# Scattering expert outputs with an add onto zero-filled rows in HBM, in place of a plain write

## The chip, the cores and the metric

The kernel runs on 1 core of one Trainium2 chip. The metric is the device time of one execution in microseconds (us), the median of the runs shown. All arithmetic is fp32; matrix products of fp32 operands are made from a high and a low part.

## The reference, cut to what matters

One layer: attention with a residual and a layer norm, then a mixture of experts with a shared expert, a residual and a layer norm. There are 2048 tokens of 512 features and 64 experts; each token goes to 6 of them, and an expert takes at most 256 rows.

```python
scores = jax.nn.sigmoid(x_flat @ w_gate)
_, topk_idx = jax.lax.top_k(scores, TOPK)                 # TOPK = 6
w = ...                                                   # scores of the six, divided by their sum
x_disp = jnp.zeros((E, CAP, C), x.dtype).at[flat_e, pos].set(x_flat[token_ids], mode='drop')
up = jnp.einsum('ecd,edh->ech', x_disp, w_up)
g_r, v_r = jnp.split(up, 2, axis=-1)
out_r = jnp.einsum('ech,ehd->ecd', jax.nn.silu(g_r) * v_r, w_down)
y_ts = jnp.where(valid[:, None], out_r[flat_e, pos_c], 0.0)
routed = (y_ts.reshape(N, TOPK, C) * w[:, :, None]).sum(axis=1)
x = _layernorm(x + shared + routed)
```

## The kernel before

**Attention and routing** (to about 1007 us). Attention runs over 8 chunks of 256 tokens. After each chunk its tokens are normalized, gated and ranked, and GpSimd (POOL) scatters each token's row (512 features and 6 codes, 518 words) into `disp_hbm`, where each expert has 256 row places; these are the 96 dispatch scatters of line 693. `disp_hbm` is zero-filled earlier, and so is `y_hbm`, the table of 12288 rows (one for each token and choice) of 512 words, in 48 transfers from `zero_hbm` (line 616).

**Experts** (about 1007 to 1242 us). The loop runs over items `n`: 6 groups of the shared expert, then the 64 experts. SyncE (SP) issues all loads on one queue (q1), in an order written out by hand (lines 626 to 640): the rows of an expert (`load_rows`, 518 KB, 8 buffers), its up weights (`load_up`, 256 KB, 20 buffers), and the down weights of two experts (`load_down`, 256 KB, 6 buffers). TensorE (PE) turns an expert's rows (`flip`, line 1589), multiplies them by the up weights (line 1391) and, for a pair of experts at a time, by the down weights (line 1637). ScalarE (ACT) and VectorE (DVE) split operands into high and low parts; POOL makes the low part of every second expert's up weights (line 776), DVE that of the others. ACT (line 960) and DVE (line 1329) copy the down product of an expert from its bank into one of four `y_out` buffers; they first wait for the scatters that last read the buffer (`y_free`, line 338).

POOL then scatters `y_out`: two instructions for an expert, 128 in all, each for 128 rows of 512 words (line 787, queue q0). The row number in `y_hbm` comes from the codes that travelled with the token; a place of the expert that holds no token has a number beyond `bounds_check` and is left out. 12288 of the 16384 places hold a token, and each number occurs once. Before its first scatter POOL waits until the zero fill of `y_hbm` is done (line 782). In POOL's own queue the scatters of a pair stand between the subtractions of line 776.

**Shared groups put off, and the end** (1234 us to the end). Two shared groups run after the experts. SP waits for all scatters (line 644), then loads the six rows of each token from `y_hbm`, 16 tiles of 128 tokens with 1536 KB each (line 648, 7 buffers). PE and DVE weight and add them (lines 1677 and 1356), and the last layer norm and the stores follow.

Of the kernel before, what the change touches and what calls it, by code (L numbers as in the profile page):

```python
# [11 lines left out]
ALU = mybir.AluOpType  # L12
# [18 lines left out]
def side_step(jobs):  # L31
    for job in jobs[:]:
        if next(job, "over") == "over":
            jobs.remove(job)


def build(nc, x, x_t, Wq, bq, Wk, bk, Wv, bv, Wo, bo, w_gate, w_sup, w_sdown, w_up, w_down, out):
# [21 lines left out]
    with ctx:  # L59
# [3 lines left out]
        def sem(name):  # L63
            return ctx.enter_context(nc.semaphore(name))
# [175 lines left out]
        d_y = [sem(f"dma_y{b}") for b in range(NY)]  # L240
# [9 lines left out]
        def outputs_at(n):  # L250

            if n >= NI - 1:
                return range(n - 1, n)
            return range(n - 2, n) if n >= SH + 2 and n % 2 == 0 else range(0)
# [52 lines left out]
        def low_by_dve(g):  # L307

            return g >= NU and g % 2 == 1
# [8 lines left out]
        def y_made(e, g, t):  # L318

            if t or g % 2:  # L320
                e.wait_ge(a_y, g + 1)
            else:
                e.wait_ge(v_y, g // 2 + 1)
# [94 lines left out]
        def split_at(n):  # L418

            g = n if n < NU else n + NU - SH if n >= SH else -1  # L420
            return range(g, g + 1) if 0 <= g < E else range(0)
# [231 lines left out]
        def gpsimd(e):  # L653
# [116 lines left out]
            for n in range(-LEAD, NI + 1):  # L770
                for g in split_at(n):
                    if not low_by_dve(g):
                        e.wait_ge(a_uphi, g + 1)
                        if g >= NU:
                            e.wait_ge(p_up, SH + g - NU + 1)
                        e.tensor_tensor(up_lo[g % NU][:, :, :], up_w[g % NW][:, :, :],
                                        up_hi[g % NU][:, :, :].bitcast(F32), ALU.subtract).then_inc(g_wlo, 1)
                side_step(jobs)
                side_step(jobs)
                for i in outputs_at(n):  # L780
                    if i == SH:
                        e.wait_ge(d_yzero, 16 * NZ)
                    g, y = i - SH, i % NY
                    e.wait_ge(v_rowat, 2 * (g // 2) + 2)
                    for t in range(2):
                        y_made(e, g, t)
                        e.indirect_dma_start(  # L787
                            y_hbm, bass.IndirectOffsetOnAxis(row_at[:, 2 * g + t:2 * g + t + 1], 0),
                            y_out[y][:, t, :], None, bounds_check=T * TOPK - 1,
                            oob_is_err=False).then_inc(d_y[y], 16)  # L790
                side_step(jobs)

            for n, part in enumerate(FINAL):
# [887 lines left out]
        block = ctx.enter_context(nc.Block())  # L1681
        block.sync(sync)
        block.gpsimd(gpsimd)
        block.scalar(scalar)
        block.vector(vector)
# [42 lines left out]
```

## Time and profile before

| | us |
|---|---|
| median of 2 runs | 1312.22 (1311.82 to 1312.63) |
| the profiled execution | 1323.67 |
| its span, first to last instruction | 1321.9 |
| PE busy, share of the span | 96% |
| DVE / ACT / POOL busy | 76% / 69% / 41% |
| read from HBM / written to HBM | 177.87 MB / 134.91 MB |

The span is what all views of the trace are counted in; a window is given in us from the span's start. A busy PE is not a PE at its peak. The DMA share is the mean busy share of the 16 DMA engines of the core. The queues are q1 for all that SP issues, q0 for the indirect transfers of POOL, q10 for the stores that ACT issues at the end. The profiled execution is longer than the median of the runs by 11.5 us, so changes of time are worked out within it.

### The profile page before, as it was taken

The page shows a single profiled execution, that of the slowest core. Times are in us where ns is not written, and L with a number is a line of the kernel's source. Part 1 is how long each engine was busy: PE and PEld are TensorE (multiplying, and loading weights), DVE is VectorE, ACT ScalarE, POOL GpSimd, SP SyncE. Part 2 cuts the span into 40 slices and gives each one's busy share as a digit, 9 for nine tenths or more (in the row PEclk, how much of TensorE's full clock was granted, in tenths as well). Part 3 has the DMA queues.
Part 4 walks back from the last instruction along what each step waited for, and adds up shares of the span by engine and source line. Part 5 has one row for each costly group of instructions (what it writes and reads, how often), then busy time and mean ns, then how long its engine had stood idle before and what let it go on. Part 6 is the DMA issues. An engine that isn't in the chain of part 4 may idle for free. (4 is left out here: it accounts for less than half of the span.)

```text
span 1321.9 us, 24272 instructions
## 1 busy us (share of the span) xinstructions
PE 1263.6 (96%) x8126; PEld 1064.1 (80%) x8126; DVE 1004.3 (76%) x1893; ACT 910.9 (69%) x1640; POOL 539.6 (41%) x537
## 2 busy tenths in 40 slices
PE   7999999999999999999999999999879999999886
PEld 5888899899899889889889889889758777777532
DVE  5623788889889889889889889979676767667377
ACT  5422598788788778778778778878624767767243
POOL 0002222324434434434434524524452877777311
PEclk9999999999999999999999999999999999999899
DMA  8789366113324324324424424435366999995597
GB/s 275 262 284 297 119 225 220 41 31 115 118 81 146 114 87 132 126 83 129 133 70 132 145 64 135 146 127 185 125 248 242 378 387 372 379 334 210 226 426 310
DMA packets 95272, 253.15 MB, mean 192 GB/s; under 512 B 17304, under 2 KB 39960, under 8 KB 91696
## 3 DMA queue, kind: packets, MB, share of 16 engines
q1 hardware_dynamic: 74928, 196.79, 43.9%
q0 software_dynamic: 17920, 50.62, 10.0%
q10 hardware_dynamic: 2304, 4.20, 0.8%
q8 instruction: 69, 1.13, 0.4%
q14 instruction: 51, 0.42, 0.1%
HBM read 177.87 MB, written 134.91 MB: 237 GB/s over the span
## 5 line engine op out<-in xcount | busy, mean ns | idle before, releaser
L901 ACT ACTIVATE p_hi<-slot 128x512 fp32r<-128x512 f32 x512 | 279.5, 596 | 113.9 <-PE slot L1526 105.8
L745 POOL TENSOR_TENSOR p_lo<-prob,p_hi 128x512 fp32r<-128x512 f32 x128 | 165.5, 1293 | 448.8 <-ACT prob L903 448.6
L1539 PE MATMUL slot<-k_stack,q_stack 128*128 128x512 f32 x1024 | 300.2, 415 | 0.0
L918 ACT ACTIVATE prob<-prob,row_min 128x1024 f32<-128x1024 f32 x256 | 296.6, 1159 | 0.1
L1240 DVE TENSOR_TENSOR p_lo<-slot,p_hi 128x512 fp32r<-128x512 f32 x384 | 251.5, 681 | 51.0 <-ACT p_hi L901 47.4
L1564 PE MATMUL pv_acc<-p_hi,v_pair 128*128 128x256 f32 x1024 | 263.1, 290 | 9.2 <-POOL p_lo L745 7.3
L1526 PE MATMUL slot<-ident,prob 128*128 128x128 f32 x2048 | 265.8, 273 | 1.3 <-ACT prob L918 1.3
L1564 PE MATMUL pv_acc<-p_lo,v_pair 128*128 128x256 f32 x1024 | 253.7, 281 | 0.0
L1526 PEld LDWEIGHTS slot<-ident,prob 128*128 128x128 f32 x2048 | 229.5, 141 | 1.9 <-issue 1.7
L1564 PEld LDWEIGHTS pv_acc<-p_hi,v_pair 128*128 128x128 f32 x1024 | 192.6, 188 | 23.4 <-issue 12.0
L1564 PEld LDWEIGHTS pv_acc<-p_lo,v_pair 128*128 128x128 f32 x1024 | 192.8, 188 | 12.9 <-issue 3.4
L1539 PEld LDWEIGHTS slot<-k_stack,q_stack 128*128 128x128 f32 x1024 | 174.0, 190 | 23.4 <-issue 0.2
L1265 DVE TENSOR_SCALAR_CACHE_REDUCE prob<-slot,row_min 128x1024 f32<-128x1024 f32 x128 | 163.2, 1276 | 1.4 <-remote 1.1
L1265 DVE TENSOR_SCALAR_CACHE_REDUCE prob<-slot 128x1024 f32<-128x1024 f32 x128 | 155.4, 1214 | 0.0
L787 POOL DMA_INDIRECT y_hbm<-y_out,row_at x128 | 132.9, 1039 | 52.1 <-issue 34.4
L1295 DVE TENSOR_TENSOR rows_lo<-slot,rows_hi 128x1024 fp32r<-128x1024 f32 x70 | 85.5, 1224 | 54.3 <-ACT rows_hi L935 37.6
L1589 PEld LDWEIGHTS slot<-ident,rows_all 128*128 128x128 f32 x576 | 65.6, 145 | 36.8 <-issue 30.7
L935 ACT ACTIVATE rows_hi<-slot 128x1024 fp32r<-128x1024 f32 x70 | 71.7, 1027 | 29.8 <-PE slot L1589 27.3
L693 POOL DMA_INDIRECT disp_hbm<-resid,scat x84 | 82.9, 987 | 21.8 <-issue 21.7
L1589 PE MATMUL slot<-ident,rows_all 128*128 128x128 f32 x576 | 78.7, 282 | 9.2 <-DMA rows_all<-disp_hbm 4.8
L960 ACT ACTIVATE y_out<-slot 128x512 f32<-128x512 f32 x64 | 48.6, 809 | 50.8 <-PE slot L1637 36.0
L903 ACT ACTIVATE prob<-slot 128x512 f32<-128x512 f32 x128 | 77.5, 606 | 0.0
(185 smaller groups left out, 2020.4 us busy)
## 6 DMA issues: line engine op xcount, KB each, us to landing
disp_hbm<-zero_hbm SPq DMA_DIRECT2D x64, 518.0 KB, 6.6
rows_all<-disp_hbm SPq DMA_DIRECT2D x64, 518.0 KB
y_hbm<-zero_hbm SPq DMA_DIRECT2D x48, 512.0 KB
got<-y_hbm SPq DMA_DIRECT2D x16, 1536.0 KB, 22.8
q_stack<-q_hbm SPq DMA_DIRECT2D x128, 128.0 KB, 3.0
up_w<-in_L_ffn_w_up SPq DMA_DIRECT2D x64, 256.0 KB
down_w<-in_L_ffn_w_down SPq DMA_DIRECT2D x32, 256.0 KB
q_hbm<-q_hi SPq DMA_DIRECT2D x8, 512.0 KB, 2.7
```

The lines of the kernel that those rows point to most:

```text
L693: e.indirect_dma_start(disp_hbm, bass.IndirectOffsetOnAxis(scat[j][:, k:k + 1], 0), sent_of_chunk(c, j), None, bounds_check=E * CAP - 1, o ...
L745: e.tensor_tensor(p_lo[1][:, 2:4, :], prob[:, m % 2, :, (4 * u + 2) * P:(4 * u + 4) * P], p_hi[1][:, 2:4, :].bitcast(F32), ALU.subtract).t ...
L787: e.indirect_dma_start(y_hbm, bass.IndirectOffsetOnAxis(row_at[:, 2 * g + t:2 * g + t + 1], 0), y_out[y][:, t, :], None, bounds_check=T * ...
L901: e.activation(p_hi[b][:, two, :], view[:, two, :], ACT.Copy).then_inc(a_phi, 1)
L918: e.activation(keys, keys, ACT.Exp, bias=row_min[:, me % 2, j, 1:2], scale=-1.0, accum_out=row_sum[:, me % 2, j, half:half + 1]).then_inc( ...
L1240: e.tensor_tensor(p_lo[b][:, two, :], view[:, two, :], p_hi[b][:, two, :].bitcast(F32), ALU.subtract).then_inc(v_lo, 1)
L1265: e.tensor_scalar(prob[:, ms % 2, j, half * HALF:(half + 1) * HALF], slot_of_take("scores", s)[:, :], -1.0 / SCALE, first, ALU.mult, ALU.m ...
L1295: e.tensor_tensor(rows_lo[f % LEAD][:, :, :], slot_of_take("flip", f)[:, :].rearrange("p (k q) -> p k q", k=KC), rows_hi[f % LEAD][:, :, : ...
L1526: made = e.transpose(view[:, t, j * P:(j + 1) * P], prob[:, m % 2, j, (4 * u + t) * P:(4 * u + t + 1) * P], ident[:, :])
L1539: made = e.matmul(slot[:, n * BANK:(n + 1) * BANK], qs[:, part, j * P:(j + 1) * P], k_stack[:, ms % H, keys], start=part == 0, stop=part == 1)
L1564: made = e.matmul(pv_acc[:, 0:QC], v_pair[:, kt, mv % H, :], src[:, t, :], start=kt == 0 and part == 0, stop=kt == NT - 1 and part == 1)
L1589: made = e.transpose(view[:, k, t, :], rows[rows_of_item(f)][:, t, k * P:(k + 1) * P], ident[:, :])
```

## The change

One operand of the scatters of line 787: `compute_op` is `ALU.add`. The transfer adds each row of `y_out` to the row that stands in `y_hbm`, in place of writing over it. The zero fill, the wait for it, the order, the buffers and all other transfers stay as they are.

```diff
                         e.indirect_dma_start(
                             y_hbm, bass.IndirectOffsetOnAxis(row_at[:, 2 * g + t:2 * g + t + 1], 0),
                             y_out[y][:, t, :], None, bounds_check=T * TOPK - 1,
-                            oob_is_err=False).then_inc(d_y[y], 16)
+                            oob_is_err=False, compute_op=ALU.add).then_inc(d_y[y], 16)
```

## Rows read from the trace of the kernel before

**Rows 1.** The page: busy time, the span in 40 slices, HBM traffic.

```profile
PE 1263.6 (96%) x8126; PEld 1064.1 (80%) x8126; DVE 1004.3 (76%) x1893; ACT 910.9 (69%) x1640; POOL 539.6 (41%) x537
...
POOL 0002222324434434434434524524452877777311
...
DMA  8789366113324324324424424435366999995597
...
HBM read 177.87 MB, written 134.91 MB: 237 GB/s over the span
```

**Rows 2.** Windows of the expert stage: us, busy time of each engine, clock, DMA share.

```profile
1007.00:1020.00 13.00, 12.88 (x91) 10.31 (x91) 10.82 (x16) 8.80 (x14) 2.54 (x2) 1.00 0.91 343
1020.00:1160.00 140.00, 134.89 (x970) 107.37 (x969) 97.41 (x161) 100.00 (x161) 110.15 (x100) 1.00 1.00 379
1160.00:1200.00 40.00, 37.98 (x274) 30.12 (x272) 28.25 (x48) 29.43 (x48) 30.82 (x29) 1.00 0.89 317
1200.00:1222.00 22.00, 21.32 (x155) 16.84 (x152) 15.68 (x26) 15.36 (x25) 16.19 (x16) 1.00 0.47 177
1222.00:1242.00 20.00, 16.47 (x82) 11.32 (x81) 4.63 (x7) 6.58 (x9) 12.45 (x13) 0.83 0.34 130
```

**Rows 3.** Waits of TensorE from 1007 to 1242 us, the longest two.

```profile
PE slot L1637 <- DVE rows_lo L1295: 4.7, 8, 0.6
PE slot L1637 <- DVE y_out L1329: 2.5, 1, 2.5
```

**Rows 4.** TensorE in order of time: the last expert tiles are turned.

```profile
1216.79 1.03 PE L1589 MATMUL slot<-ident,rows_all 128*128 128x128 f32 x8
```

**Rows 5.** Windows up to the last turn, and from it to the stage's end.

```profile
1007.00:1217.00 210.00, 202.08 (x1448) 161.00 (x1448) 147.34 (x240) 150.67 (x240) 157.21 (x143) 1.00 0.94 351
1217.00:1242.00 25.00, 21.47 (x115) 14.96 (x114) 9.45 (x14) 9.50 (x14) 14.93 (x16) 0.86 0.31 119
```

**Rows 6.** DMA queues: first from 1007 to 1217, then from 1007 to 1242.

```profile
q1 hardware_dynamic: 19264, 51.23, 66.5%
q0 software_dynamic: 8960, 22.21, 26.8%
...
q1 hardware_dynamic: 19264, 51.23, 59.4%
q0 software_dynamic: 10240, 25.17, 27.2%
```

**Rows 7.** GpSimd in order of time, then all scatters of both lines.

```profile
1060.98 1.32 POOL L776 TENSOR_TENSOR up_lo<-up_w,up_hi 128x512 fp32r<-128x512 f32 x1
...
1063.78 0.97 POOL L787 DMA_INDIRECT y_hbm<-y_out,row_at  x1 [0.30 <-issue]
...
1067.30 1.32 POOL L776 TENSOR_TENSOR up_lo<-up_w,up_hi 128x512 fp32r<-128x512 f32 x1
...
1073.72 1.30 POOL L776 TENSOR_TENSOR up_lo<-up_w,up_hi 128x512 fp32r<-128x512 f32 x1
1076.08 0.99 POOL L787 DMA_INDIRECT y_hbm<-y_out,row_at  x1 [1.06 <-ACT y_out L960]
...
1081.44 1.31 POOL L776 TENSOR_TENSOR up_lo<-up_w,up_hi 128x512 fp32r<-128x512 f32 x1
...
L787 POOL DMA_INDIRECT y_hbm<-y_out,row_at x128: 972/973/1747, 1020.9 to 1239.7; - x128
...
L693 POOL DMA_INDIRECT disp_hbm<-resid,scat x84: 967/975/1200, 306.0 to 957.0; - x84
```

**Rows 8.** The last scatter; SyncE's waits; its wait instruction at L644.

```profile
1239.68 0.97 POOL L787 DMA_INDIRECT y_hbm<-y_out,row_at  x1 [0.30 <-issue]
...
SPq L316 <- POOL up_lo L776: 35.6, 18, 3.0
...
L644 SPq EVENT_SEMAPHORE  x2: 28/3848/7667, 1234.6 to 1242.3; - x2
```

**Rows 9.** The chain that ended last, from the gather on.

```profile
1255.22 21.74 DMA got<-y_hbm
```

## The prediction

> **What bounds the kernel now.** I read the page first [rows 1]: TensorE (PE) is busy 96% of the span and GpSimd (POOL) 41%, but the fourth of the span that holds the expert scatters (from slice 31 on) looks different. There POOL stands at 7 or 8 tenths where it had 2 to 5 before, and the DMA engines stand at 9 tenths for five slices in a row. So the average over the span says nothing here, and I cut the stage out by windows [rows 2]. Four stretches are to be seen. From 1007 to 1020 us the pipeline fills. From 1020 to 1160 PE is busy 134.89 of 140 us and the DMA share is 1.00. From 1160 to 1200 PE is still full, but the DMA share falls to 0.89, and from 1200 to 1222 to 0.47. Then the experts drain and the last two shared groups run, PE at 16.47 of 20 us. From 1242 the gather of the scattered rows runs.
>
> The order of work on PE sets the pace of the experts: it waits on other engines for some 7 us in the whole stage [rows 3]. But the DMA engines are only a little behind. Two engines are to be looked at next, since the changed instruction is issued on one and carried out on the other.
>
> The DMA engines first. The last two expert tiles are turned (L1589) at 1216.79 us, so all expert loads have landed by 1217 [rows 4]. From 1007 to 1217 the DMA share is 0.94, that is 197 of 210 us on each engine [rows 5]; 13 us are free. Of it the load queue (q1) has 66.5%, 139.7 us for 51.23 MB, and the scatters (q0) 26.8%, 56.3 us for 22.21 MB [rows 6]. The 8960 packets of the scatters are 80 for each of 112 of the 128 scatters; the other 16 come after 1217. q1 moves all of its 51.23 MB by 1217: the window that ends at 1242 has the same sum. Loads run ahead of PE as far as buffers allow, which is why the share is 1.00 first and falls later: PE's pace, not DMA, ends the stage, with 13 us in hand.
>
> POOL second. A scatter takes 973 ns and is followed by 0.30 us of issue, so 1.28 us from one to the next [rows 7]. A pair of experts has four, and one subtraction (L776, 1.3 us) on POOL. In the rows that subtraction stands at 1060.98, 1067.30, 1073.72 and 1081.44 us: a pair takes 6.3 to 6.4 us where POOL waits for nothing, and 7.7 where ScalarE's (ACT) copy to y_out comes late. From the first scatter at 1020.9 us to 1217 there are 112 of them, 28 pairs, 7.0 us each; so POOL has some 0.65 us to spare in a pair, 0.16 us for each scatter.
>
> The last wait of the stage is SyncE's (SP): it waits at L644 for the scatters until 1242.3 and then issues the gathers [rows 8]. The last scatter begins at 1239.68 and takes 0.97 us, so it lands at most 1.7 us after its issue ended. From there the chain is the gather at the DMA engines' pace (its first piece on the chain, got from y_hbm, is 21.74 us) and a short tail [rows 9]. Those 79 us start later if the scatters land later, and are otherwise untouched.
>
> **The change, step by step.** It removes nothing and adds no instruction, no wait and no byte of y_out. Each of the 128 scatters (L787) now asks for an add to what stands in y_hbm. The zero fill (48 transfers, L616) and its wait at L782 are there already. Each valid row is hit once, so nothing is added twice.
>
> 1. *Engine time of a scatter.* An add needs the old row. The trace has no accumulating transfer, so I bound it. From below: nothing, if the add takes place at the memory or if the second read runs beside the first. From above: every packet of a row pair waits for a full round trip, at most the 1.7 us of the last scatter [rows 8]; with 4 such packets to an engine in a scatter, 128 x 4 x 1.7 = 870 us. Between these ends lies a second read of the same bytes. Its price is in the rows: as much as the scatter itself takes now, 56.3 us up to 1217, or, at the loads' price, 22.21 MB x 139.7/51.23 = 60.6 us [rows 6]. I take this middle value, since the rows that it is nearest to are transfers of the same 2 KB rows on the same engines, and since nothing suggests that packets run one by one (q0 and q1 together fill the engines to 1.00 [rows 2]).
>
> What this gives: 56.3 to 60.6 us more work on each engine by the time that the last expert tiles are turned, less the 13 us that are free, is +43.3 to +47.6 us. The cover that hides the scatters now, the PE work of the pairs, is used up: for each of the 28 pairs scattered by 1217 the engines would have (139.7 + 2 x 56.3)/28 = 9.0 us of work, where the stretch has 210/28 = 7.5. The loads that are late then are those of the rows of the experts (64 loads of 518 KB) and of their weights; both stand in SP's one queue. PE waits for them at the turn (L1589). Of q1's loads, the two of x1 rows (2 of 512 KB, 2.9 us) aren't needed by then, which takes up to 2.9 us off. I take +43.5 us.
>
> The Trainium skill, "Collectives: The Full Stack", section "The bandwidth ceiling: the fold count and why AG ≠ RS ≠ AR", says that a reducing transfer emits two reads for one write on the same ring, and that this halves its rate (measured ratio 1.93). No row here shows a reducing transfer. By its 1.93 the scatters' 56.3 us would grow by 52.4 us, and the sum would be 4 us lower than by the value of the rows.
>
> 2. *Issue on POOL.* 128 instructions, of which the trace shows only the plain form, 973 ns. From below nothing. From above I double it, +0.97 us, for an instruction that writes twice the descriptors; three descriptors where there were two would be half of it, +0.49 us. With +0.49 a pair on POOL takes 6.35 + 4 x 0.49 = 8.3 us, which is under the 9.0 us of the DMA engines. I take it as hidden under step 1: what costs most is a bound on the same pairs, and the two don't add. Behind the scatters on POOL stand the subtraction L776, and for it PE's expert matmuls and SP's next weight load (L316, 35.6 us of waits now, all of it for buffers that are filled ahead of need [rows 8]).
>
> 3. *Buffers of y_out.* ACT and VectorE write y_out again two pairs later, some 14 us, after the scatters landed. POOL needs 5.1 us of that to issue a pair's four, and the transfers 2 x 2.0 = 4 us of engine time, twice as long beside loads, 8 us. That just fits, and where it doesn't, the wait falls into the same DMA-bound pairs. Nothing.
>
> 4. *The end of the stage.* After 1217 the DMA share is 0.31 [rows 5], 16 scatters are left, and 8 us more work in 25 us doesn't bind. The last scatter lands later by its own second read: 22.21 MB are 5422 packets of two rows, 56.3 us on 16 engines makes 0.17 us for each, and 4 of them on an engine are +0.7 us [rows 6]. The gather is unchanged, so are attention and the dispatch scatters (L693), which aren't edited.
>
> Sum: +43.5 + 0.7 = +44 us. The profiled execution took 1323.67 us, of which 1321.9 is the span, so it would be 1368. The median of the runs is 1312.22, 11.5 us lower; the same +44 gives 1356.
>
> **Rivals.**
> A. *Second read* (forecast): 1356 us, between 1340 and 1372 as the price of the second read lies between 0.8 and 1.3 of the scatter's own.
> B. *Hidden* (the other side): the add costs the engines little, since the second read overlaps or is done at the memory. Place: the DMA engines from 1007 to 1217. The price of it is 56.3 us x (f - 1), f being the new engine time over the old, and it decides up to f = 1.23, where the 13 us are used up: 1312 to 1314 us. For it: the old rows are all zero and never needed by anything else, and HBM traffic, both ways, stands at only 237 GB/s over the span [rows 1]. Against it: the engines, not HBM, are full.
> C. *Issue on POOL or a dearer add*: either POOL takes +0.97 us, a pair 6.35 + 3.9 = 10.2 us, 30 pairs 3.2 us longer each, +97 us; or the add runs the engine at a third of its rate, 2 x 56.3 - 13 = +100 us. Both give about 1410 us. For POOL: it has only 0.16 us to spare for a scatter. Against: the dispatch scatters, with 518 elements to a row in place of 512, take the same 975 ns [rows 7], so what a row carries doesn't enter.
> D. *One by one*: packets that read, add and write in series. 870 us instead of 64 us on the engines, beside 139.7 of loads: 139.7 + 870 - 210 is +800, about 2110 us; with overlap of a few packets, something between 1460 and that. The Trainium skill, "DMA: Bandwidth & Descriptors", section "Two DMAs through the same engine are not ordered", tells of two such packets on one queue of which the second read stale data when it directly followed, which speaks for overlap and against this one; no row here shows it.
> That the flag changes nothing on the chip would be B too, by another way, with q0's row as it was.
>
> **How the numbers follow.** A 0.44, B 0.20 (with all that ends under +26 us, which is f below 1.7), C 0.23, D 0.13. Faster has no mechanism and gets 0.01 out of B for an effect of order. The predicted time is that of A, 1356 us. The range leaves out D and the upper part of C: 1311 to 1425 us. A alone would be 1340 to 1372. Within 2% (26 us, about what a measurement of this kernel can tell from no change) lies the rest of B: 0.19; faster 0.01; slower 0.80.
>
> **What would show it.** Step 1: q0's share of the stage about doubles in us, while q1's bytes stay 51.23 MB; the DMA share is 1.0 up to the last turn; PE in the stage waits at L1589 on rows_all from disp_hbm, and PE's busy share falls from 0.96 to 0.8. HBM read grows by 25 MB. Step 2: L787 at 973 ns, or up to 1.46 with PE's waits still on DMA; if PE waits for up_lo and y_out with a DMA share under 0.9, it was C. If the stage from 1007 is no longer than 235 us, it was B. If q0's packets take over 1 us each, D. The time from SP's L644 to the end stays at 79 us in all.

## The result

The changed kernel takes 1397.12 us (median of 2 runs, 1395.99 to 1398.24) against 1312.22 before: 1.0647 times as long, 95% interval 1.0601 to 1.0693, or +84.9 us. A later set of runs on another occasion gave 1.065 (1.0632 to 1.0668). The direction was as forecast; the size was +44 there. The profiled executions differ by less than the medians: 1323.67 before and 1395.99 after, +72.3 us. I come back to these 12.6 us, since they are part of the miss. The measured 1397 us lies between forecast A (1356, with a span of its own from 1340 to 1372) and rival C (about 1410), and nearer to C.

The page of the changed kernel, the lines that answer to [rows 1], with q0 of its part on DMA queues:

```profile
PE 1279.6 (92%) x8126; PEld 1073.3 (77%) x8126; DVE 1008.2 (72%) x1893; ACT 911.4 (65%) x1640; POOL 614.1 (44%) x537
...
POOL 0003223345244244344344345254378878788511
...
DMA  8788464124244244243243244356599999998797
...
q0 software_dynamic: 26112, 50.64, 15.8%
...
HBM read 177.87 MB, written 134.91 MB: 224 GB/s over the span
```

The DMA row stands at 9 for seven slices in a row where it did for five. q0 had 17920 packets, for the same bytes (50.62 MB) and 10.0% of the engines. The traffic counters did not move: if the add fetches the old rows, neither the packets' bytes nor the HBM reads show it.

The last expert tiles are turned, as [rows 4]:

```profile
1282.09 1.03 PE L1589 MATMUL slot<-ident,rows_all 128*128 128x128 f32 x8
```

The stage in two windows, as [rows 5]: up to the last turn of expert tiles, now at 1282, and from there to the end of the scatters; then the queues in the first of them, as [rows 6].

```profile
1007.00:1283.00 276.00, 217.54 (x1443) 169.86 (x1442) 152.84 (x239) 150.60 (x239) 221.81 (x143) 0.94 1.00 266
1283.00:1315.00 32.00, 24.89 (x134) 17.95 (x132) 11.13 (x17) 11.50 (x22) 23.46 (x16) 0.89 0.72 96
```

```profile
q1 hardware_dynamic: 19186, 50.91, 52.9%
q0 software_dynamic: 16065, 22.12, 47.0%
```

The stretch that took 210 us takes 276, and the DMA share over it is 1.00; the 13 us that were free are gone. TensorE's granted clock has a mean of 0.94 in the stretch, where it was 1.00, the upper of its two levels. That is not what sets the pace: a_less and b_issue2 below keep 0.98 and 0.99 in most of the stage and are slow all the same. q1 has 146.0 us for its 51 MB (139.7 before), q0 has 129.7 us for 22.1 MB (56.3 before). So +73.4 us for the scatters, +6.3 for loads that got a little dearer beside them, less the 13 that were free, is +66.7, and the stretch grew by 66. A scatter that took 80 packets now takes 144. Both counts fit 16 engines with 8 rows and one end packet each, two rows to a packet before and one now. By its packets q0 carried 16065/144 = 112 scatters in the stretch, as before. The engine time of one went from 0.503 to 1.16 us, a factor of 2.31.

GpSimd in order of time, and the changed instruction over the whole stage, as [rows 7]:

```profile
1070.32 1.87 POOL L776 TENSOR_TENSOR up_lo<-up_w,up_hi 128x512 fp32r<-128x512 f32 x1
1072.36 1.55 POOL L787 DMA_INDIRECT y_hbm<-y_out,row_at  x1 [0.17 <-issue]
1074.22 1.78 POOL L787 DMA_INDIRECT y_hbm<-y_out,row_at  x1 [0.30 <-issue]
...
1079.17 1.88 POOL L776 TENSOR_TENSOR up_lo<-up_w,up_hi 128x512 fp32r<-128x512 f32 x1
...
1088.18 1.87 POOL L776 TENSOR_TENSOR up_lo<-up_w,up_hi 128x512 fp32r<-128x512 f32 x1
...
L787 POOL DMA_INDIRECT y_hbm<-y_out,row_at x128: 1542/1549/2398, 1018.4 to 1309.5; - x128
```

A scatter takes 1549 ns where it took 973, and one follows the other after 1.85 us. A pair of experts takes 8.9 to 9.0 us on GpSimd, which here waits for nothing: it is full too. Over the whole stage it is not quite: it waits 20.3 us for the copies to y_out and for TensorE, and a pair takes 9.5 us on average.

The waits from 1007 to 1315 us, first of TensorE (us in total, times, longest), then of ScalarE:

```profile
PE slot L1589 <- DMA rows_all<-disp_hbm: 35.1, 22, 2.2
PE slot L1637 <- DVE rows_lo L1295: 22.4, 12, 3.1
...
ACT y_out L960 <- PE slot L1637: 49.8, 31, 2.9
ACT y_out L960 <- DMA y_hbm<-y_out,row_at: 43.7, 18, 3.8
```

TensorE now waits where the forecast put it, at the turn, for expert rows from HBM; [rows 3] had no such wait. ScalarE waits 43.7 us for scatters to land before it may write y_out again, which did not occur before.

The chain of work that ended last shows where in the stage each of the two holds it up, here the last load of expert rows on it, what follows at once, and the longest piece after that; then the window from 1240 to 1280 us:

```profile
1202.51 24.88 DMA rows_all<-disp_hbm
...
1230.04 1.55 POOL y_hbm L787
...
1269.40 11.16 DMA y_hbm<-y_out,row_at
```

```profile
1240.00:1280.00 40.00, 31.37 (x205) 23.62 (x202) 21.40 (x37) 20.62 (x33) 35.07 (x24) 0.93 0.92 218
```

Up to about 1228 us the chain goes mainly through the loads of expert rows, with a DMA share of 1.02. From 1230 to the end of the scatters it goes mainly through GpSimd's scatters and their landing, and the share falls to 0.92. So the loads set the pace for some 220 us, and the issue and return of the scatters for the last 80.

At the end, SyncE's wait at L644, as the last line of [rows 8]: it is over at 1314.7 in place of 1242.3, +72.4 us.

```profile
1309.49 1.55 POOL L787 DMA_INDIRECT y_hbm<-y_out,row_at  x1 [0.30 <-issue]
...
L644 SPq EVENT_SEMAPHORE  x2: 28/5426/10825, 1303.8 to 1314.7; - x2
```

The +72.4 us come apart as: last turn at 1282.09 in place of 1216.79, +65.3; from there to the last scatter 27.4 us in place of 22.9, +4.5, as its scatters are issued 1.85 us apart in place of 1.28; from the last scatter to the end of the wait 5.2 in place of 2.6, +2.6. From the end of that wait to the end both traces take 79.6 us.

### The profile page after: what moved, and what is told of

It reads as the page before. It is cut to its first block and busy times, and to the rows that moved or that the text cites. A ratio compares the mean times of both kernels' runs of the same rounds, so it can differ in the third digit from the quotient of the medians.

```text
span 1394.3 us, 24272 instructions
## 1 busy us (share of the span) xinstructions
PE 1279.6 (92%) x8126; PEld 1073.3 (77%) x8126; DVE 1008.2 (72%) x1893; ACT 911.4 (65%) x1640; POOL 614.1 (44%) x537
## 3 DMA queue, kind: packets, MB, share of 16 engines
q0 software_dynamic: 26112, 50.64, 15.8%
HBM read 177.87 MB, written 134.91 MB: 224 GB/s over the span
## 5 line engine op out<-in xcount | busy, mean ns | idle before, releaser
L787 POOL DMA_INDIRECT y_hbm<-y_out,row_at x128 | 206.0, 1609 | 52.0 <-issue 31.7
L1564 PEld LDWEIGHTS pv_acc<-p_hi,v_pair 128*128 128x128 f32 x1024 | 192.6, 188 | 23.6 <-issue 13.5
L1589 PEld LDWEIGHTS slot<-ident,rows_all 128*128 128x128 f32 x576 | 67.2, 148 | 77.9 <-DMA rows_all<-disp_hbm 55.3
L1589 PE MATMUL slot<-ident,rows_all 128*128 128x128 f32 x576 | 82.0, 289 | 45.5 <-DMA rows_all<-disp_hbm 41.6
L1637 PE MATMUL slot<-down_w,hid 64*128 64x512 f32 x256 | 70.4, 661 | 22.4 <-DVE rows_lo L1295 22.4
## 6 DMA issues: line engine op xcount, KB each, us to landing
down_w<-in_L_ffn_w_down SPq DMA_DIRECT2D x32, 256.0 KB, 22.9
```

What stands on the lines that cost most here:

```text
L787: e.indirect_dma_start(y_hbm, bass.IndirectOffsetOnAxis(row_at[:, 2 * g + t:2 * g + t + 1], 0), y_out[y][:, t, :], None, bounds_check=T * ...
L1564: made = e.matmul(pv_acc[:, 0:QC], v_pair[:, kt, mv % H, :], src[:, t, :], start=kt == 0 and part == 0, stop=kt == NT - 1 and part == 1)
L1589: made = e.transpose(view[:, k, t, :], rows[rows_of_item(f)][:, t, k * P:(k + 1) * P], ident[:, :])
```

## The experiments

Theory "engines": the DMA engines' extra work sets the new pace. Theory "issue": GpSimd's 1549 ns does. The trace above has both full, so it can't tell. The runs came in three sets, each beside the kernel before on the same chip, but each set on a chip of its own (7, 0 and 11). One thing is needed to read them: the kernel before stood at 1325.95 us in the first set and at 1312.97 and 1311.83 in the other two. The variant with the moved subtraction does not share that shift: 1397.77 in the first set, 1393.73 in the third. The changed kernel itself was not run in the first set; it took 1397.12 and 1397.68, both times with the kernel before at 1312. I therefore compare variants of the changed kernel with its 1397 us, within some 4 us between sets. Its repetition in the third set can't decide the question that it was made for, since the kernel before stood at 1312 there once more:

> The changed kernel again, unedited, beside the three others of this set, because the kernel before has stood at 1313 us in one set of runs and at 1326 in another. If the changed kernel doesn't share that shift, it stays at 1395 to 1399 us whatever the kernel before takes beside it; if it does, it moves by some 13 us with it.

| variant | us | ratio to before (95% interval) |
|---|---|---|
| **set 1**, before 1325.95 | | |
| b_issue: plain, small multiply | 1329.23 | 1.002 (1.0006 to 1.0033) |
| b_move: plain, more transfers | 1386.92 | 1.0452 (1.0435 to 1.0469) |
| a_dve: add, GpSimd relieved | 1397.77 | 1.0541 (1.0523 to 1.0559) |
| a_less: add, fewer loads | 1384.25 | 1.043 (1.0413 to 1.0448) |
| **set 2**, before 1312.97 | | |
| a_both: both reliefs | 1366.74 | 1.0409 (1.0387 to 1.043) |
| b_issue2: plain, larger multiply | 1363.21 | 1.0383 (1.0362 to 1.0403) |
| b_im2: plain, both imitations | 1382.36 | 1.0526 (1.0505 to 1.0547) |
| a_alt: add in every other pair | 1351.81 | 1.0298 (1.0277 to 1.032) |
| **set 3**, before 1311.83 | | |
| after2: the changed kernel again | 1397.68 | 1.065 (1.0632 to 1.0668) |
| a_dve2: add, GpSimd relieved | 1393.73 | 1.0625 (1.0607 to 1.0643) |
| a_half: add, 256 columns | 1376.67 | 1.0495 (1.0478 to 1.0513) |
| b_half: plain, 256 columns | 1309.21 | 0.9975 (0.9964 to 0.9985) |

### Imitating the issue cost on the kernel before

First with a multiply of 128x1 elements ahead of each scatter:

```diff
+                        e.tensor_tensor(pad[:, 2 * g + t:2 * g + t + 1], zeros[:, 0:1], zeros[:, 0:1], ALU.mult)
                         e.indirect_dma_start(
```

> The kernel before, with one small GpSimd multiply (128x1, nearest row 0.60 us for 128x2) put ahead of each of the 128 plain scatters: the issue cost of the add (1549 against 973 ns) without its transfers. Output as the reference. Theory 'issue' (GpSimd sets the pace of the changed kernel): a pair of experts goes from 7.0 to 6.35 + 4 x 0.6 = 8.8 us or a little more, 32 pairs, so +55 to +75 us over the kernel before, most of the +85. Theory 'engines' (the DMA engines' extra work alone explains it): GpSimd has slack that this uses up, and the loss is under +25 us.

The multiply took 0.21 us in most places, and the gap ahead of the scatter shrank from 0.30 to 0.16 us: scatters came 1.39 us apart in place of 1.28. The dose was a fifth of what was wanted, and the loss was 3.3 us. All that this says is that a pitch of 1.39 costs next to nothing. So again with a larger one, chained by a semaphore:

```diff
+                        e.wait_ge(g_pad, 2 * g + t)
+                        e.tensor_tensor(pad[:, :], zeros[:, 0:1].to_broadcast([P, 168]),
+                                        zeros[:, 0:1].to_broadcast([P, 168]), ALU.mult).then_inc(g_pad, 1)
```

> The kernel before with a larger GpSimd multiply (128x168) ahead of each plain scatter. The first try of this (128x1) ran in 0.21 us and hid half of that in the gap ahead of the scatter, so it added 0.1 us where the add costs 0.58. Wanted is a pitch of about 1.85 us from scatter to scatter as in the changed kernel. Output as the reference. If GpSimd's issue alone sets a bound 13 us under that of the engines, the loss is 8.9 to 9.0 us for a pair against 7.0, +50 to +62 us (ratio 1.038 to 1.047). If GpSimd's issue isn't a bound, under +15 us (1.011).

+50.2 us. GpSimd of this kernel, in order of time:

```profile
1058.83 1.28 POOL L778 TENSOR_TENSOR up_lo<-up_w,up_hi 128x512 fp32r<-128x512 f32 x1
1060.06 0.47 POOL L790 TENSOR_TENSOR pad<-zeros 128x168 f32<-128x168 f32 x1
1060.69 1.01 POOL L792 DMA_INDIRECT y_hbm<-y_out,row_at  x1 [0.17 <-POOL pad L790]
1061.73 0.48 POOL L790 TENSOR_TENSOR pad<-zeros 128x168 f32<-128x168 f32 x1
...
1067.34 1.27 POOL L778 TENSOR_TENSOR up_lo<-up_w,up_hi 128x512 fp32r<-128x512 f32 x1
...
1076.04 1.28 POOL L778 TENSOR_TENSOR up_lo<-up_w,up_hi 128x512 fp32r<-128x512 f32 x1
```

The pitch is 1.68 us, still 0.17 short of the changed kernel's, and a pair takes 8.5 to 8.7 us in these rows, 8.4 on average over the stage. With plain scatters, no byte more and a DMA share of 0.91 from 1020 to 1200 us and less behind it, GpSimd's issue alone costs 50 us. Scaled to 9.0 us for a pair, (9.0 - 7.0)/(8.6 - 7.0) x 50 = 62 us, or 71 with 8.4 in place of 8.6; these are estimates. Issue is a real bound, and not a small one.

### Imitating the engines' work on the kernel before

```diff
+                if n >= SH:
+                    for t in range(2):
+                        e.dma_start(more_hbm[2 * (n - SH) + t], zero_hbm[:, 0:512]).then_inc(d_more, 16)
```

> The kernel before, with 128 more transfers (two for each expert, 256 KB from HBM to HBM, 2 KB pieces, 84 ns each on an engine) issued by SyncE between the loads: about 86 us more work on each DMA engine, near the 89 us that the adding scatters brought (152.8 against 64.0 us), and nothing on GpSimd. Output as the reference. Theory 'engines': 86 - 13 free = +60 to +75 us over the kernel before. Theory 'issue': the loads run far enough ahead that it costs under +25 us. If each alone gives +50 or more, the two are bounds of about the same height, and neither alone is the cause.

+61.0 us, as the theory of the engines has it. The waits of TensorE in this kernel's stage, longest first:

```profile
PE slot L1595 <- DMA rows_all<-disp_hbm: 47.9, 31, 2.9
PE slot L1595 <- DMA rows_all<-x_hbm: 13.8, 1, 13.8
```

The first is the same wait as in the changed kernel (L1595 is the turn here). The extra transfers also take SyncE time to issue, 656 ns each (L637), which the adding scatters don't. But the DMA share is 1.02 from 1020 to 1240 us, so the engines were full all the same. The 61.0 us are against the kernel before at 1326; if transfers that bind hide its shift, as they seem to do in the changed kernel, it would be 74 us against 1313. Each of the two costs alone is thus worth 50 us or more. Both together:

> The kernel before with both imitations: the multiply ahead of each scatter and the 128 extra transfers of SyncE (86 us on each engine). Output as the reference. If the two are parallel bounds, the time is that of the larger one alone, near b_move's ratio of 1.045 or up to 15 us more, and near the changed kernel's 1.054. If they add up, +110 to +125 us (ratio 1.085 or more).

+69.4 us. In its own set that is 19 us more than the issue alone (b_issue2). Beside the transfers alone it is 0.7% more in ratio and 4.6 us less in time; the two were in different sets. By either count they do not add up (50 and 61 would give 111): these are two bounds on the same pairs. The changed kernel stands 15 us above this one. The pitch here is shorter by 0.17 us, which is some of it; the rest was not parted.

### Relieving one side of the changed kernel

The subtraction of L776 goes to VectorE for all experts from the fifth on:

```diff
         def low_by_dve(g):
-            return g >= NU and g % 2 == 1
+            return g >= NU
```

> The changed kernel with the subtraction of line 776 moved from GpSimd to VectorE for all experts from the fifth on (output as the reference). It takes 1.85 + 0.17 - 0.30 - 0.2 = about 1.5 us from GpSimd's 9.0 us for a pair, and leaves the transfers as they are. Theory 'issue': a pair falls to 7.5 us and the kernel is 35 to 48 us faster than the changed one (about 1350 to 1362). Theory 'engines': the loads still arrive as late, under 12 us faster (over 1385).

> The changed kernel with the subtraction of line 776 on VectorE, once more, now beside the changed kernel. Theory 'engines set the pace, issue stands a little lower': within 4 us of the changed kernel. Theory 'issue': 15 us faster or more.

Beside the changed kernel it is 4 us faster (1393.73 against 1397.68), in the first set it was level with it. GpSimd was busy 221.81 us from 1007 to 1283 and is now 181.14, and the stretch is as long:

```profile
1007.00:1283.00 276.00, 216.54 (x1454) 169.95 (x1454) 163.95 (x271) 151.89 (x240) 181.14 (x115) 0.96 1.00 265
```

The DMA share stays at 1.00. VectorE got that work, 163.95 us busy of 276, and a_both below gains with the same move, so it is not what holds this kernel up. So the engines are the higher of the two bounds. Next, only a quarter of each late weight load (some experts are computed with the weights of others):

```diff
+            ks = slice(0, KC if g < NW else 1)
-            e.dma_start(up_w[b][:, :, :], w_up[g]).then_inc(d_up[b], 16)
+            e.dma_start(up_w[b][:, ks, :], w_up[g][:, ks, :]).then_inc(d_up[b], 16)
```

> The changed kernel with a quarter of each load of up weights from the 21st expert on, and of down weights from the 13th on (so those experts are computed with the weights of others, and the output isn't the reference's): 44 loads of 256 KB and 26 of 256 KB shrink to a quarter, 13.8 MB or 38 us less on each DMA engine, GpSimd unchanged. Theory 'engines': 30 to 38 us faster than the changed kernel (1359 to 1367). Theory 'issue': under 12 us faster.

1384.25 us, 13 us faster than the changed kernel, and 13.5 us faster than a_dve, which ran in the same set. That is neither of the two answers that were written down (30 to 38, or under 12). The waits of this kernel say why:

```profile
ACT y_out L962 <- DMA y_hbm<-y_out,row_at: 103.2, 52, 3.9
...
PE slot L1591 <- DVE rows_lo L1297: 28.8, 23, 2.0
```

TensorE's wait for expert rows is gone from the list of its longest; ScalarE's wait for y_out has more than doubled, since GpSimd, back to back at 8.85 us for a pair, sends the buffers off that slowly. In the chain that ended last, from 990 to 1315 us, the loads of expert rows fell from 38.4% to 2.6%, and GpSimd's scatters rose from 20.2% to 32.1%. The kernel fell 13 us, down to the bound of issue, and stopped. If so, the two reliefs together must give more than their sum:

> The changed kernel with both reliefs at once: the subtraction on VectorE and the smaller weight loads (some experts get the weights of others, so the output isn't the reference's). Alone the first gave nothing (1.054 times the kernel before, as the changed kernel by its own trace) and the second about 13 us. Theory 'engines, with issue a little lower': the smaller loads gave only 13 us because GpSimd's 8.9 us for a pair then set the pace; with that lifted the other 25 us appear, 30 to 40 us faster than the changed kernel, ratio 1.023 to 1.032 to the kernel before. Rival 'return of y_out' (ScalarE waits for the scatters to land, whatever GpSimd and the loads do): no faster than with the smaller loads alone, ratio 1.040 or more.

1366.74 us, 31 us faster than the changed kernel, where the sum of the single gains is 13 + 4 = 17. In absolute time this is what was expected of the theory "engines, with issue a little lower". Its ratio (1.0409) lies outside the 1.023 to 1.032 that I had written beside it and on the rival's side. I had worked these ratios out from a kernel before at 1326, and it stood at 1313 here; the traces, which do not depend on it, have spans of 1383.8 us with the loads alone and 1365.2 with both. I read them for the theory, but a_less and a_both were not in one set. In the trace of a_both ScalarE still waits 43.0 us for scatters to land, so the return of y_out takes a share that these runs do not measure by itself. More y_out buffers would need another layout of the buffers, and weren't tried.

### Half as many adds

```diff
-                            oob_is_err=False, compute_op=ALU.add).then_inc(d_y[y], 16)
+                            oob_is_err=False, **({'compute_op': ALU.add} if g % 4 < 2 else {})).then_inc(d_y[y], 16)
```

> Every other pair of experts scatters with an add, the rest with a plain write (output as the reference). Theory 'engines': half of the extra work, 0.5 x 1.39 x 56.3 = 39 us up to the last turn, less the 13 us that are free, and the tail: +26 to +32 us (ratio 1.020 to 1.024). A loss in proportion to the number of adds, with no slack used up first, would be half of +72: +36 us (ratio 1.027).

+38.8 us by medians, more than either number. Against the profiled execution of the kernel before, the span grew by 27.2 us (1349.1), which is the answer of the engines with slack used up first. Which of the two holds depends on the 12.6 us below, and this run alone doesn't decide it.

### What an add costs by the byte and by the row

Both kernels leave out half of each expert's output:

```diff
+        y_half = y_hbm[0:T * TOPK // 2, :].rearrange('r (h n) -> (r h) n', h=2)
...
-                            y_out[y][:, t, :], None, bounds_check=T * TOPK - 1,
+                            y_out[y][:, t, 0:C // 2], None, bounds_check=T * TOPK - 1,
```

> The changed kernel with each adding scatter cut to the first 256 of 512 columns, onto half rows that lie one behind the other (half of each expert output is left out, so the output isn't the reference's). It parts what an add costs by the byte from what it costs by the row. By the byte (a second read at the rate of the first): a packet of 193 ns falls to about 100, q0 from 153 to about 80 us on an engine, and the engines stop to bind. By the row: the packet stays over 150 ns. GpSimd's issue: 1549 ns if it goes by the number of rows, less if by bytes. With engines freed and issue as it was, GpSimd's 8.9 us for a pair sets the pace: 8 to 14 us faster than the changed kernel.

> The kernel before with each plain scatter cut to 256 columns in the same way (output isn't the reference's). The plain packet of two rows falls from 161 ns to about 84, q0 from 64 to about 33 us, issue stays 973 ns. The engines had time in hand already, so the time stays within 4 us of the kernel before; if it falls by more, the engines were a bound in the kernel before too.

The scatter instruction of the half-width add, then q0 from 1007 to 1283 in it, then q0 from 1007 to 1242 in the half-width plain kernel:

```profile
L788 POOL DMA_INDIRECT y_hbm<-y_out,row_at x128: 1542/1549/2362, 1016.9 to 1290.7; - x128
```

```profile
q0 software_dynamic: 17568, 12.17, 33.1%
```

```profile
q0 software_dynamic: 6144, 12.60, 14.2%
```

The issue stays at 1549 ns to the nanosecond with half the bytes: it goes by rows. On the engines, 33.1% of 276 us for 17568/144 = 122 scatters is 0.75 us each, against 1.16 at full width. Halving the bytes took off 0.41, so the bytes of a full row set cost 0.83 us and 0.34 us are there whatever the width; the packets stayed at 144. For the plain write the same subtraction gives 14.2% of 235 us over 128 scatters, 0.26, against 0.50: 0.48 us for the bytes, 0.02 fixed. But the plain write's packets fell with its bytes, from 80 to 48 (6144/128, which fits four rows to a packet), so its 0.48 us holds whatever a packet costs. As an estimate, then, the add makes what goes by width dearer by 0.35 us (1.7 times, less than a full second read; more than 1.7 by the byte, if packets cost something) and brings about 0.31 us a scatter that doesn't go by width, some 50 ns for each of the six valid rows that an engine has in it. Whether that is the row itself or its packet isn't parted. Neither of my two answers was right: it is both, in nearly equal shares, as far as this subtraction can tell. The packets ran beside loads, so these are prices in this mix.

The half-width add is 21 us faster than the changed kernel, with GpSimd at 8.6 us for a pair: again down to the bound of issue (in its chain from 990 to 1315 us, GpSimd's scatters have 36.3% and the loads of expert rows 1.5%). I had expected 8 to 14; what the other 7 us are, beyond lighter scatters after the last load, isn't shown. The half-width plain kernel gains 2.6 us: the engines were hardly a bound in the kernel before, as forecast.

## Why the prediction was right, and where it was short

**The bound and its place: right for most of the stage.** The DMA engines are the higher bound (a_dve2 against a_less), TensorE waits at L1589 for rows from disp_hbm, the 13 us of slack are used up, and the gather is untouched (79.6 us in both). But the last 80 us of the stage hang on GpSimd's scatters and their landing. No step of the forecast had that.

**The number: less good than it looks.** The range of 1311 to 1425 us was wide because it took in most of rival C. A alone had 1340 to 1372, and the measured 1397 is 25 us beyond it. The way was right, and the size was +84.9 us where +44 was forecast.

**Step 1, the price of the add: mis-sized.** "I take this middle value", a second read at 56.3 to 60.6 us, should have been 73.4 us. The factor is 2.31 and not 2. That is 1.30 times the scatter's own price, the upper end of what I had allowed A. The part by width was less than I gave it (0.35 us a scatter where I took 0.50); what I had not priced is the part by rows or packets, 0.31 us. I had the clue to it: 80 packets for 128 rows means two rows in a packet, and I never asked whether an add could still be packed so. With 73.4 and the 6.3 us by which the loads became dearer the step gives +66.7, and the last turn came 65.3 us later. That is 22 us over the +43.5 of this step. That an add reads the old rows at all isn't shown by any counter; the runs show its engine time alone.

**Rival C, a third of the rate or a dearer issue (+100 us).** By time it is the nearest of the four, but neither of its forms came. The engines run a scatter at 1/2.31 of the rate and not at a third, and an instruction takes GpSimd 0.58 us more and not 0.97.

The Trainium skill, "Collectives: The Full Stack", section "The bandwidth ceiling: the fold count and why AG ≠ RS ≠ AR", has the rate halved by the second read. This case's traces give a factor of 2.31 at rows of 2 KB, the part by width 1.7; the measurement decides.

**Step 2, issue hidden: right by a hair, while there are loads.** It took +0.58 us, more than the +0.49 of the nearer estimate and less than the doubled bound. A pair is 9.0 us on GpSimd against 9.8 of engine work ((146.0 + 129.7)/28 = 9.8). Taking the subtraction off GpSimd gained 4 us at most. But I called it a thing that costs nothing, and it would have cost 50 us or more had the transfers been free: rival B, "hidden", was therefore no case of +0 at all. Its price left out the issue bound on the same pairs.

**Step 3, y_out: "Nothing" was wrong as a forecast of the trace.** ScalarE waits 43.7 us for scatters. Some of it lies in pairs that wait for loads anyway. But the chain that ended last runs through landing scatters too, for 8.1% of 990 to 1315 us or 26 us, of which the last scatter has 5. How much of it would be gained by more buffers stays open.

**Step 4, the end: too small.** +0.7 us was the second read of the last scatter alone. The last eight or more scatters are issued 1.85 us apart and land behind one another: +4.5 and +2.6 us, 7.1 in all. After the last turn there is no load left to be late for, so there the issue cost isn't hidden by anything. Its cover ended with the loads, and I didn't say so.

**From the trace to the median: short by 12.6 us.** In the traces the sum was 1368 and the execution took 1395.99: 28 us short, 22 by step 1 and 6 by step 4. Another 12.6 us come from carrying a difference between profiled executions over to medians. The kernel before ran at about 1312 or at about 1326, and its profiled execution (1323.67) is near the upper level, while the medians that the result is held against are at the lower. No such shift was seen in the changed kernel or its variants. No trace of the unedited kernel before at the lower level exists here. The nearest is b_half, in a set where it stood at 1311.83: its scatters are over at 1228.5, 13.8 us earlier than in [rows 8], and nearly all of its pairs take 6.6 to 6.7 us, without the late y_out copies of [rows 7], where the kernel before takes 7.1 on average. Its lighter scatters may be some of that.

```profile
L645 SPq EVENT_SEMAPHORE  x2: 28/3848/7667, 1220.8 to 1228.5; - x2
```

That suggests that the levels lie in the expert stage, and that a kernel bound by the engines wouldn't show them. At the lower level the stage would then be some 13 us shorter for the same 197 us of engine work. The 13 us that I counted as free would not exist, which is nearly the 12.6 us. It is an estimate. The only set at 1326 was also the only one on chip 7, so the level may belong to the chip; what makes it isn't shown.

**What would show it.** q0's time doubled and more, and the share of 1.00 and the wait at L1589 came as listed. q1's bytes were 50.91 MB up to the last turn, near the 51.23. PE's busy share fell to 0.79 (217.54 of 276), as said. HBM reads did not grow by 25 MB in the counters. That sign failed, and it stays open whether no old row was fetched or the counters leave it out.

## What to carry to other kernels

A flag on a transfer can change three prices at once: what the issuing engine takes for each row, how many rows share a packet, and what the DMA engines take for the bytes. Price each against its own slack, since on a stage with several engines near the bound the dearest sets the time, and relieving only that one brings you down to the next (here 13 us of the 38 that the smaller loads were worked out to free). Where a cost is called hidden, say until when: behind the last load nothing hid it. And before a difference between traces is added to a median, see that the profiled execution stands at the level of the median.

## What the runs showed of the hardware

- An adding indirect scatter of 128 rows takes GpSimd 1549 ns, a plain one 973 ns, and at 1 KB a row in place of 2 KB they are the same (1549 and 975).
- A plain scatter took 80 packets at 2 KB a row and 48 at 1 KB, which fits two and four rows to a packet; an adding one took 144 at both, one row to a packet. At 2 KB a scatter took 0.50 us on an engine plain and 1.16 us with the add, beside the loads of this stage.
- No counter shows old rows being read for an add: q0's bytes and the HBM reads are those of the plain kernel (50.64 against 50.62 MB, 177.87 MB in both).
